# Two stretches of feed-forward rounds in a macaron kernel: written out, or as loops on the chip

## The reference

```python
x = x + 0.5 * ffn(layernorm(x))      # "half": 2 layers
x = x + attn(layernorm(x))           # 16 heads over all 512 tokens, then one projection
x = x + 0.5 * ffn(layernorm(x))      # the same half again, same weights

def layer(x, ...):                   # one of the 2 layers of ffn
    q, k, v = split(shift_token(x) @ wqkv)            # 8 heads of 64
    q, k = rotary_xpos(l2norm(q) * qs, l2norm(k) * ksc)
    x = x + local_attention(q, k, v) @ wo             # each block of 128 tokens sees itself and the one before
    a, g = split((layernorm(shift_token(x)) * lg + lb) @ w1 + b1)
    return x + (a * gelu(g)) @ w2 + b2
```

## Time and profile before

| | us |
|---|---|
| median of three runs (lowest, highest) | 3730.74 (3728.74, 3733.53) |
| the profiled execution, its own time | 3728.74 |
| its span, first to last instruction | 3727.0 |
| TensorE busy | 3454.1 |
| VectorE busy | 2637.5 |
| GpSimd busy | 2269.1 |
| ScalarE busy | 2078.0 |
| mean granted TensorE clock, share of full speed | 0.974 |

### The profile page before, as it was taken

One profiled execution on the slowest core, in us unless ns is written; L12 is line 12 of the kernel. 1 busy time (PEld: TensorE's weight loads), 2 busy tenths in 40 slices (PEclk: granted clock), 3 DMA queues, 4 the chain that ended last, 5 costly groups with the idle time before them and its releaser, 6 DMA issues.

```text
span 3727.0 us, 69799 instructions
## 1 busy us (share of the span) xinstructions
PE 3454.1 (93%) x21152; PEld 2830.3 (76%) x21152; DVE 2637.5 (71%) x7104; ACT 2078.0 (56%) x4840; POOL 2269.1 (61%) x2307
## 2 busy tenths in 40 slices
PE   4799998899999699999999999996999989899997
PEld 2578777777877588888888888884778777677775
DVE  6687877788888465565555655656787877788884
ACT  2475775567677244444444444443676667567663
POOL 3567666657766355555555555574577666667762
PEclk9899999999999899999999999998999999999998
DMA  4444344434435431222212212204344335434433
GB/s 138 135 151 134 118 153 129 136 105 154 153 118 162 107 73 45 44 52 57 46 46 47 58 51 46 69 18 127 123 141 149 113 126 161 132 120 151 155 113 106
DMA packets 425513, 397.17 MB, mean 107 GB/s; under 512 B 139292, under 2 KB 373416, under 8 KB 425128
## 3 DMA queue, kind: packets, MB, share of 16 engines
q1 hardware_dynamic: 425128, 392.57, 35.0%
HBM read 224.67 MB, written 159.38 MB: 103 GB/s over the span
## 4 chain that ended last, share of the span: by engine, by line
PE 69%; DVE 11%; issue 7%; ACT 7%; POOL 3%; DMA 2%; SPq 1%; DVEq 0%; ACTq 0%; POOLq 0%
PE psum L1446 19%; PE psum L1447 18%; PE psum L1448 18%; PE psum L1582 5%; PE psum L1554 3%; PE psum L1668 3%; ACT probs L910 3%; DVE probs L1152 2%; PE psum L1565 2%; POOL ge_lo L809 1%; DVE ssq L1132 1%; DVE p_blocks L1174 1%; DVE nT_lo L1219 1%; ACT L931 1%; DVE nb L1160 1%
## 5 line engine op out<-in xcount | busy, mean ns | idle before, releaser
L809 POOL TENSOR_TENSOR ge_lo<-ge,ge_hi 128x512 fp32r<-128x512 f32 x512 | 672.7, 1316 | 527.2 <-PE psum L1448 285.1
L770 POOL TENSOR_SCALAR probs<-probs,rz 128x256 f32<-128x256 f32 (+1 forms) x1024 | 447.0, 456 | 518.8 <-DVE rz L1166 518.8
L983 ACT ACTIVATE ge<-psum 128x512 f32<-128x512 f32 x512 | 307.1, 600 | 668.1 <-PE psum L1668 665.9
L1343 DVE CAST ge_hi<-ge 128x512 fp32r<-128x512 f32 x512 | 269.1, 528 | 502.1 <-ACT ge L983 497.4
L910 ACT ACTIVATE probs<-probs,nb,rq 128x256 f32<-128x256 f32 (+1 forms) x1024 | 576.1, 567 | 50.4 <-DVE nb L1160 49.3
L745 POOL TENSOR_TENSOR rinv<-ssq,minus_half 128x16 f32<-128x16 f32 x124 | 366.5, 2956 | 21.1 <-DVE ssq L1136 14.4
L1152 DVE CUSTOM_DVE_ANT_0 probs<-psum,mask 128x256 f32<-128x256 f32 (+1 forms) x1024 | 336.7, 385 | 47.7 <-PE psum L1565 37.2
L1446 PE MATMUL psum<-wqkv_hi,hT_hi 128*128 128x512 f32 x768 | 339.0, 441 | 26.3 <-issue 16.8
L1174 DVE STREAM_TRANSPOSE p_blocks<-probs 128x384 f32<-128x384 f32 (+1 forms) x384 | 291.1, 784 | 65.6 <-POOL probs L770 61.5
L1446 PE MATMUL psum<-nT_hi,w_hi 128*128 128x512 f32 x704 | 291.0, 413 | 30.7 <-ACT gate L931 23.6
L1447 PE MATMUL psum<-wqkv_hi,hT_lo 128*128 128x512 f32 x768 | 312.9, 407 | 0.0
(11 more groups left out here) (153 smaller groups left out, 9795.2 us busy)
## 6 DMA issues: line engine op xcount, KB each, us to landing
p_turned<-p_blocks SPq DMA_DIRECT2D x128, 512.0 KB, 2.8
pT<-p_turned SPq DMA_DIRECT2D x512, 128.0 KB, 3.0
p_turned<-p_blocks SPq DMA_DIRECT2D x128, 384.0 KB, 2.6
pT<-p_turned SPq DMA_DIRECT2D x512, 96.0 KB, 2.5
xnext<-stream SPq DMA_DIRECT2D x32, 512.0 KB, 3.9
xmid<-stream SPq DMA_DIRECT2D x32, 512.0 KB, 3.9
gaT<-y_turned SPq DMA_DIRECT2D x256, 64.0 KB, 2.0
y_turned<-probs SPq DMA_DIRECT2D x192, 64.0 KB, 2.9
```

Of the source, the lines that this page charges most:

```text
L770: last = nc.gpsimd.tensor_scalar(pu, pu, rz[:, h, t:t + 1], 1.0, ALU.mult, ALU.mult)
L809: nc.gpsimd.tensor_tensor(ges[1][:, k % 4, :], ge[:, k % 4, :], f32(ges[0][:, k % 4, :]), ALU.subtract).then_inc(S["g_lo"], 1)
L983: nc.scalar.activation(ge[:, k % 4, :], RB[k % 2], ACT.Exp, scale=GSCALE, accum_out=gz[:, h, t:t + 1]).then_inc(S["g_exp"], 1)
```

## The change

The two Python loops become `eng.Fori`, the loop on the chip, on every engine:

```diff
--- before.py
+++ after.py
@@ -370,11 +370,11 @@
         a_round(n0, prev=False, load=2 * call)
         a_round(n0 + 1, early=2 * call + 1)
         a_round(n0 + 2)
-        for j in range(B - 4):
+        with eng.Fori(0, B - 4) as j:
             a_round(n0 + 3 + j)
         a_round(n0 + B - 1, switch=2 * call + 1)
         a_round(n0 + B, load=2 * call + 1, layer=1)
-        for j in range(B - 2):
+        with eng.Fori(0, B - 2) as j:
             a_round(n0 + B + 1 + j, final=B * (call + 1), layer=1)
         a_round(n0 + ROUNDS - 1, nxt=False, final=B * (call + 1), layer=1)
         last(n0 + ROUNDS - 1, B * (call + 1))
```

## The result

The changed kernel takes **3782.3 us** (median of four runs, 3778.1 to 3786.3) where the kernel before took 3729.7 (four runs, 3724.9 to 3733.5): a ratio of 1.0141, with a 95% interval of 1.0124 to 1.0160. It is 53 us slower. The forecast was 3732, with a range up to 3752; it was wrong.

A forecast was written before the change was run, and what follows sets the result against it. PE's own work bounds the kernel (67.81 of each 69.1 us); 3728.7 + 1 for register work + 0 for jumps, 0 to 1 for `xnext`, gave 3730; with the median 2.0 above the profiled run, 3732 us, range 3721 to 3752.

The forecast's parts named there:

- The jump's cost: At the 16 jumps back on each engine: 0.3 us taken for a jump, hidden by idle time, 0 in the sum.
- rival C: VectorE's loop body is fetched again at every turn: about +36 us, 3768 us; chance 0.07.
- C's size: Per VectorE miss 2.7 us in layer 0, 3.4 in layer 1, less about 0.8; one badly placed loop +7 to +13.
- VectorE's jump where it hits: Before `X0`: 0.4 us, hidden by idle time before `zl` or given back by PE's 0.8 us wait; 0, else 2 us.
- Register work: Some 40 register instructions on PE, 55 on VectorE a round: +0.05 us a round, +1 us; upper bound +38.
- rival D: Slower by register instructions, a quarter of the upper bound paid: 0.5 us a round, +10, 3741 us; chance 0.13.
- PE's and SP's jumps: PE's jump before `Q2`, SP's before its fetch of `xnext`: 0.3 us each, hidden, cost 0 at the median.
- Rival B: PE's block store does not hold 962 instructions: each jump stops PE 0.9 us, +14, 3746 us; chance 0.08.
- `xnext`: SP's fetch for PE's transposes: 0.6 of 1.0 us slack used, 0 at the median; slow landings cost 1 us in all.
- Fetches: Fewer instruction fetches needed, which took 0.3% and 0.1% of the DMA engines: counted 0.
- The signs to look for: In the changed kernel's profile: looped round's period, branch times, idle time before `zl`, and new names among PE's waits.

The follow-up runs named there:

- E1: The changed kernel with VectorE's four loop heads padded to the start of a 128-instruction fetch block: 3744.7 us, 1.0046 to the kernel before.
- E2: The changed kernel with VectorE's four loop heads placed at slot 111 of a fetch block, bodies across four blocks: 3814.4 us, 1.0234 to the kernel before.
- E7: The kernel before, no loops, with three unused memsets (some 3.1 us) on VectorE ahead of `X0` in the 20 rounds: 3765.2 us, ratio 1.0103.
- E5: The changed kernel with only VectorE looped, heads at a fetch block's start, other engines written out: 3739.6 us, 1.0028 to the kernel before.
- E6: The kernel before, no loops, with one unused memset (some 0.5 us) on VectorE ahead of `X0` in the 20 rounds: 3729.1 us, ratio 1.0002.
- E3: The changed kernel with VectorE's rounds written out, the other four engines looped: 3740.9 us, 1.0037 to the kernel before.
- E8: E2 with an instruction at the head of each VectorE turn that names the jump's target in advance: 3758.3 us, 1.0084 to the kernel before.
- E9: The changed kernel, heads not moved, with the instruction that names VectorE's jump target in advance: 3752.4 us, 1.0068 to the kernel before.

## Why the prediction was wrong

- **The jump's cost, the step that failed.** "DVE's 275 or 277 take three blocks, or four if the loop's head falls in the last fifth of one." That was right but for the size of the fifth, and the text then went on with 0.3 us for every loop. "I take 0.3" was written of PE, for which it held; of VectorE only the good case was ever put into the sum. By E1 and E2 the place decides: three blocks return in 0.3 us, four miss. Loops 1 and 4 were placed badly, their jumps took 2.8 to 4.1 us, and each missed jump cost 4.4 to 4.7 us of time; this is rival C in half of its places. As to the fifth: of 128 places 18 are bad for a body of 275 and 20 for 277, one in seven. Four heads with one chance in seven each have at least one bad place in about half of all cases (estimate, with the places taken as independent: 0.48; by my own one in five, 0.59), and I gave C 0.07. A condition that held in one case of seven was priced as if it never held.
- **C's size.** "About 2.3 x 16 = +36", and "+7 to +13" for one loop. Loop 1 cost 12.6 us for 3 misses, loop 4 26.0 and a part of the 4.1 behind it for 5; by E1, a missed jump costs 4.4 to 4.7 us, twice my 2.3. Three terms were wrong or missing. The wait that comes last is not the one I watched: "What is late next is `zl`", but PE's `z0` waits for the first half of `X0` (E7; the slack is 1.8 and 0.6 us, not 0.9 and 0.2). "Less about 0.8 that the later wait gives up": the gelu's wait gave up nothing in any round read (0.8 in all). And the lower clock was not thought of: some 1.6 us a round in loop 4.
- **VectorE's jump where it hits.** "`zl` and `j1` come 0.2 us late, and PE's 0.5 us wait becomes 0.7": it became 0.8 (E5), 0.7 in loop 2. "But the chain to the 0.8 us wait does not run through `j1`, so that wait shrinks by as much": wrong. PE is `n`'s engine too, and everything behind it, the gelu's input included, moves with it; the wait stays. The 2 us that stood behind "if it does not" was the right bound for this term.
- **Register work.** "+0.05 us a round" is wrong for layer 1, where a round with clean jumps takes 0.5 to 0.6 us more in E5 and E1 (0.2 to 0.3 in layer 0). It is what rival D asked for, 0.5 a round, with its reason: VectorE has no lag there. E6 parts it: to be 0.4 us late at `X0`, as by the jump alone, costs 0 to 0.2. The register instructions make it 0.63 at `X0` and 0.73 at `nb`: 0.2 us go at `z0`'s weight load, whose slack is used up, and 0.33 at PE's wait for the normalised rows. The comparison with the attention misled, as the text had feared: its engines run several steps behind one another.
- **PE's and SP's jumps.** Right: 0.27 to 0.40 us on PE at every turn of every run, SP 0.3 to 0.4. Rival B is refuted: 962 instructions, four or five of PE's larger blocks, stay. `xnext` came closer than forecast. SP fetches it 0.8 to 0.9 us later before `z0` (0.6 was forecast), and in every second clean round of layer 1 of the changed kernel and E1 the profile ends `z0`'s idle weight load, 0.3 to 0.4 us, with its landing. The rounds between idle as long with the landing 0.2 us earlier, and E5, whose SP is not looped, idles 0.26 to 0.30 for `X0`; so at most 0.1 us of it can be `xnext`.
- **Fetches.** "I count 0" for having fewer of them: right. PE's queue fetched 119 blocks in E3, and its looped rounds took 69.2 us, no less than before.
- **The signs to look for** were right and sufficient: "over 2 us on DVE is C", "a new name among PE's waits". They named the cause.

The Trainium skill ("Runtime: NRT & Kernel Launch", Instruction fetch mechanics) warned that a taken branch outside the kept window forces a fetch and stalls, and the runs agree: 2.8 to 4.6 us for each. The prediction read its window of 2 cache lines as two blocks of 8.2 KB, by which VectorE would have missed everywhere, and E1's 16 jumps over three blocks took 0.3 us. But the page's lines are of 16 KiB, 256 instructions each, and two of them would have held 275 or 277 instructions from most places. What the runs show on q14 is a block of half that size, 8.2 KB, of which three stay (E1) and four don't (E2); the measurement decides. The section also says that prefetch is purely sequential. No plain jump here speaks against it, and E8 shows the exception, a hint by which four blocks return in 0.3 us, and behind which the code that follows the loop comes late.

## What to carry to other kernels

Here a loop on the chip saved code, not time, and its price depended on where its head falls among the fetch blocks: count the blocks that each engine's body touches with the real place of the head, or pin the head or hint the jump, before trusting it. Both had a price of their own: some 1.4 us for each entry over the padding that missed, and a stop of 1.8 to 2.5 us behind each loop. Price each condition by its chance instead of taking the case that holds more often, above all where several places draw the same lot. And to find what a late engine delays first, look for who waits for the buffers that it frees, not only for its own next operation.

## What the runs showed of the hardware that I had not expected

- Of VectorE's instructions, without a hint, three blocks of 8.2 KB stay at hand and a body of four does not: 0.3 us against 3.2 to 4.6 a jump, and 70 us over 16 jumps (E1, E2). Each miss brings some five blocks (187 and 231 for 148).
- A missed jump can be more than one wait: 3.2 to 4.5 us before `X0`, and another 0.67 to 1.23 where the head's block ends 12 or 15 instructions on (the changed kernel); 0.1 to 0.4 where it ends after 17 (E2).
- BRANCH_PREFETCH_HINT (39 ns) took the miss from every jump, without a fetch in its place (151 blocks for 231), and left one stop of 1.8 to 2.5 us behind each loop (E8, E9).
- TensorE's granted clock stayed at 1.00 when PE waited 2.2 and 0.7 us behind each other (E7), and went down to 0.50 for 3.4 us after 2.7 and 1.8 us (loop 4 of the changed kernel). In its loop 1, 2.6 and 1.1 us left it at 1.00, and 3.1 or 2.7 us at `z0` alone brought it down. In E2, with 2.9 to 3.4 us at `z0`, it fell in 15 of 16 rounds.
